# Causal self-attention on one core: the mask of the first score pass moved from TensorE to VectorE

## What is computed

```
x = _layernorm(x + _L0_attn_ref(x, L0_attn_Wq_down, ...), axis=-1)
```

## Time and profile before

| | |
|---|---|
| median of 3 runs | 2562.7 us (2561.79 to 2567.87) |
| profiled execution: time | 2562.45 us |
| profiled execution: span from the first to the last instruction | 2560.6 us |
| mean granted TensorE clock | 0.878 of full speed |
| TensorE matmuls busy | 2133.6 us (83%) |
| VectorE busy | 1537.1 us (60%) |
| ScalarE busy | 949.2 us (37%) |
| GpSimd busy | 926.3 us (36%) |
| the self-attention stage | from 0 to about 404 us of the span |

### The profile page before, as it was taken

The page is one execution under the profiler, slowest core; times in us unless marked ns, Lnnn a source line. Parts: engine busy times, 40 slices in busy tenths (PEclk is TensorE's granted clock), DMA queues, the critical chain, the costliest instruction groups (busy, mean ns, idle before and its releaser), DMA issues. The chain is left out here.

```text
span 2560.6 us, 58413 instructions
## 1 busy us (share of the span) xinstructions
PE 2133.6 (83%) x20310; PEld 1601.6 (63%) x20310; DVE 1537.1 (60%) x3500; ACT 949.2 (37%) x1881; POOL 926.3 (36%) x911
## 2 busy tenths in 40 slices
PE   5999997999776664888399996899999999997575
PEld 4666665777676563665398885566666666664233
DVE  0344443555454455333244654699999999984798
ACT  0444442333211110333124341344444444442797
POOL 0111111111144545232554531355555555553333
PEclk9999998999887776899677887899999999997555
DMA  6011003656311110876322311011000110000111
GB/s 207 26 30 30 29 25 116 217 198 215 132 50 32 37 35 24 271 241 182 92 86 78 102 39 39 26 32 32 26 28 30 32 32 30 24 20 8 53 57 46
DMA packets 157644, 192.76 MB, mean 75 GB/s; under 512 B 28517, under 2 KB 141160, under 8 KB 157559
## 3 DMA queue, kind: packets, MB, share of 16 engines
q1 hardware_dynamic: 136426, 179.73, 22.5%
q10 hardware_dynamic: 10861, 9.30, 1.2%
q0 software_dynamic: 10272, 2.62, 0.5%
HBM read 140.74 MB, written 77.51 MB: 85 GB/s over the span
## 5 line engine op out<-in xcount | busy, mean ns | idle before, releaser
L2730 ACT ACTIVATE xa_prob<-xa_A 121x1600 f32<-121x1600 f32 x96 | 144.5, 1505 | 304.2 <-PE xa_A L2609 304.2
L2801 POOL TENSOR_TENSOR xa_prob<-xa_prob,xa_exp_bias 121x1600 f32<-121x1600 f32 x64 | 228.7, 3574 | 41.0 <-ACT xa_prob L2730 40.9
L2908 DVE TENSOR_REDUCE xa_kq<-xa_A 100x4 f32<-100x1444 f32 x128 | 211.6, 1653 | 20.8 <-PE xa_A L2582 20.6
L1408 POOL DMA_INDIRECT slot_rows<-rt_x_again,rt_slot_u x150 | 151.9, 1012 | 163.8 <-DVE rt_x_again L1526 102.1
L2888 DVE TENSOR_SCALAR xa_rows_n<-xa_rows_t,xa_mv,xa_rstd 121x256 f32<-121x256 f32 x128 | 142.4, 1172 | 2.4 <-POOL xa_rstd L2818 2.4
L2609 PEld LDWEIGHTS xa_A<-xa_q2T,xa_kqT 17*121 17x121 f32 x3072 | 93.8, 185 | 56.5 <-DVE xa_kq L2908 35.9
L2582 PE MATMUL xa_A<-xa_kqT 16*100 16x361 f32 x1024 | 112.9, 510 | 10.0 <-ACT xa_prob L2730 6.8
L2609 PE MATMUL xa_A<-xa_q2T,xa_kqT 17*121 17x100 f32 x3072 | 109.3, 280 | 13.8 <-DVE xa_kq L2908 13.2
L695 DVE TENSOR_REDUCE sa_kq<-sa_A 100x16 f32<-100x1600 f32 x32 | 58.5, 1827 | 102.8 <-PE sa_A L453 102.8
L1654 POOL DMA_INDIRECT contrib<-ex_y,ex_place_u x64 | 62.4, 975 | 154.3 <-ACT ex_y L1706 135.5
L2823 POOL TENSOR_TENSOR xa_o_rstd<-xa_o_var,xa_power 100x1 f32<-100x1 f32 x32 | 17.9, 560 | 252.1 <-DVE xa_o_var L2948 252.1
(11 more groups left out here) (345 smaller groups left out, 5439.6 us busy)
## 6 DMA issues: line engine op xcount, KB each, us to landing
ex_w<-in_w13T SPq DMA_DIRECT2D x64, 352.0 KB
contrib<-xs_zero SPq DMA_DIRECT2D x30, 640.0 KB
la_rows<-contrib SPq DMA_DIRECT2D x16, 1200.0 KB
xs_ctxT<-in_ctxT SPq DMA_DIRECT2D x32, 512.0 KB
xa_rows_t<-in_ctx SPq DMA_DIRECT2D x96, 121.0 KB
ex_w<-in_w2T SPq DMA_DIRECT2D x64, 176.0 KB
slot_rows<-xs_zero SPq DMA_DIRECT2D x32, 272.0 KB
ex_x_t<-slot_rows SPq DMA_DIRECT2D x64, 136.0 KB, 2.2
```

The lines of the kernel that those rows point to most:

```text
L1408: nc.gpsimd.indirect_dma_start(slot_rows, bass.IndirectOffsetOnAxis(slot_u[:, k, n:n + 1], 0), x_again[:, k, :], None, bounds_check=SLOTS ...
L2730: nc.scalar.activation(prob[:, n, :].rearrange("p (h a) -> p h a", h=HPG), A[:ROWS, :, 0:G * T], ACT.Exp, scale=EXP_SCALE).then_inc(exp_re ...
L2801: nc.gpsimd.tensor_tensor(chunk, chunk, exp_bias[:, n, :].unsqueeze(1).to_broadcast([ROWS, HEADS, T]), ALU.mult).then_inc(biased, 1)
L2908: nc.vector.tensor_reduce(kq[:T, k, NCH, 4 * j:4 * j + 4, DH:DH + 1].rearrange("p h o -> p (h o)"), A[:T, :, 0:src_len], axis=AXIS_X, op=A ...
```

## The change

The four constant products L448 of the first pass go; its 16 score products overwrite the banks (`start=True`). VectorE adds a mask of 100 x 100 in float32 (`later_keys`, 0 or -1e30) to the 1600 columns while it copies them out of the banks to a new tile `masked` in SBUF (`mask`), and `maxima` reduces `masked` in place of the banks. A new semaphore `masked_ready` says that the banks have been read; `score_turned` waits for it in place of `max_ready`. `maxima` now stands behind `rope` in VectorE's body. One more constant is loaded at the start (19 DMAs in place of 18). The second pass keeps its four constant products.

```
--- before.py
+++ after.py
@@ -290,6 +290,8 @@
+        later_keys = s.sb("later_keys", [T, T])
+        masked = s.sb("masked", [T, HPG, G * T])
@@ -334,7 +336,7 @@
-        W_ALL = 16 * 18
+        W_ALL = 16 * 19
@@ -372,6 +374,7 @@
                 sp.dma_start(causalf[:], w["causal"]).then_inc(w_in, 16)
+                sp.dma_start(later_keys[:], w["later_keys"]).then_inc(w_in, 16)
                 rows((0, 0))
@@ -444,14 +447,11 @@
                     pe.wait_ge(kqT_ready, at(b, 2, 2))
                     pe.wait_ge(exp_ready, at(later(b, -2), 1, 1))
-                    for h in range(HPG):
-                        nc.tensor.matmul(A[:T, h, 0:G * T].rearrange("p (j t) -> p j t", t=T), causal[:],
-                                         identb[:].unsqueeze(1).to_broadcast([T, G, T]), start=True, stop=False, skip_group_check=True)
                     for j in range(G):
                         for h in range(HPG):
                             part = slice(32 * h, 32 * h + DH)
                             last = nc.tensor.matmul(A[:T, h, j * T:(j + 1) * T], kqT[part, k, j, T:2 * T], kqT[part, k, j, 0:T],
-                                                    start=False, stop=True, skip_group_check=True)
+                                                    start=True, stop=True)
                     last.then_inc(scored, 1)
@@ -470,7 +470,7 @@
                     if scores_between:
-                        pe.wait_ge(max_ready, at(later(b, 1), 1, 1))
+                        pe.wait_ge(masked_ready, at(later(b, 1), 1, 1))
@@ -688,12 +688,18 @@
+                def mask(b):
+                    dve.wait_ge(scored, at(b, 1, 1))
+                    dve.wait_ge(max_ready, at(later(b, -1), 1, 1))
+                    nc.vector.tensor_tensor(masked[:].rearrange("p h (j t) -> p h j t", t=T), A[:T, :, 0:G * T].rearrange("p h (j t) -> p h j t", t=T),
+                                            later_keys[:].unsqueeze(1).unsqueeze(1).to_broadcast([T, HPG, G, T]), ALU.add).then_inc(masked_ready, 1)
+
                 def maxima(b):
                     k = b[1] % 2
-                    dve.wait_ge(scored, at(b, 1, 1))
+                    dve.wait_ge(masked_ready, at(b, 1, 1))
                     dve.wait_ge(q2_turned, at(later(b, -2), 1, 1))
                     nc.vector.tensor_reduce(kq[:, k, 1, :, DH:DH + 1].rearrange("p (j h) o -> p j (h o)", j=G),
-                                            A[:T, :, 0:G * T].rearrange("p h (j t) -> p j h t", t=T),
+                                            masked[:].rearrange("p h (j t) -> p j h t", t=T),
                                             axis=AXIS_X, op=ALU.max).then_inc(max_ready, 1)
@@ -730,9 +736,11 @@
                     if has(-3):
                         finish(later(b, -3))
                     if has(1):
-                        maxima(later(b, 1))
+                        mask(later(b, 1))
                     if has(2):
                         rope(later(b, 2))
+                    if has(1):
+                        maxima(later(b, 1))
                     if has(-1):
                         divide(later(b, -1))
@@ -3484,6 +3492,7 @@
+    c["later_keys"] = np.where(t[None, :] <= t[:, None], 0, NEG).astype(np.float32)
```

More of the change, by code:

```diff
@@ L327, in self_attention @@
         kq_turned, kqT_ready = s.sem("kq_turned"), s.sem("kqT_ready")
-        scored, max_ready = s.sem("scored"), s.sem("max_ready")
+        scored, masked_ready, max_ready = s.sem("scored"), s.sem("masked_ready"), s.sem("max_ready")
         q2_turned, q2_ready = s.sem("q2_turned"), s.sem("q2_ready")
@@ L675, in _ @@
                 nc.vector.memset(kq[:, :, 0, :, DH:DH + 1], -1.0).then_inc(cleared, 1)
-                for sem, per in ((roped, 1), (max_ready, 1), (rec_ready, 1), (y_ready, 1), (r_ready, 1), (o_stats_ready, 1), (o_mv_ready, 1),
+                for sem, per in ((roped, 1), (masked_ready, 1), (max_ready, 1), (rec_ready, 1), (y_ready, 1), (r_ready, 1), (o_stats_ready, 1), (o_mv_ready, 1),
                                  (o_var_ready, 1), (out_ready, 1)):
```

## The result

| | before | changed |
|---|---|---|
| median of five runs | 2562.7 us (2556.24 to 2669.53) | 2539.56 us (2531.96 to 2543.56) |
| profiled execution, span | 2560.6 us | 2537.5 us |
| mean granted TensorE clock | 0.878 | 0.874 |
| ratio of the runs | | 0.9906 (95% interval 0.9884 to 0.9928) |

The run of 2669.53 us was in a slower state of the chip, which the ratio leaves out; the other four of the kernel before end at 2567.87. The change saves 0.9%, 23.1 us between the two medians as between the two spans. The forecast was 25.5 us, 2537 us. Run again beside the kernel before on another occasion, the changed kernel came to 0.9903 (0.987 to 0.9937).

The account below looks back on a forecast made before the run. The prediction took TensorE's instructions, one behind another, as the bound: -25.9 us for the products and +0.4 for the start make -25.5, from 2562.45 to 2537 us, with a range of 2533 to 2547.

Parts of the forecast that it names:

- The bound and the two places: Stage loop: TensorE, 95% busy, sets the pace; it waits before L465, and L477's two inputs come due within 0.1 us.
- The products that go: First pass on TensorE: the four constant products take 0.81 us per batch, 25.9 us less over 32 batches.
- The mask at 1.83 us: VectorE's new addition of 1600 columns takes 1.83 us, between 1.80 and 2.15, so L477 waits as before.
- The maxima at 1.80 to 1.83 us: VectorE's maxima, read from SBUF behind rope, fill 1.80 us of idle time; L702 is delayed by less than 0.1 us.
- The 0.8 us of cover: VectorE's queue behind the maxima: L713 ends 0.8 us before the second half of L439 needs its bank.
- The start, +0.4 us: Stage start: one more constant's DMA delays TensorE's first work by 0.4 us.
- The wait that stays: TensorE's 0.48 us wait for ScalarE before L465 moves with the period, neither won nor lost.
- The first batch: The four products take 1.50 us there; 0.81 was counted, the 0.7 of difference kept for the range.
- The mask was not slow: Rival, 4%: VectorE's addition takes about 3.4 us, L477 waits 1.6 us more per period; 26 us worse, 2589 us.
- The clock did not fall: Rival, 2%: TensorE's clock drops in the loop, some 8 us more per affected period; eight periods would make 2601 us.
- No gain came back as a wait: Rival, 4%: the 0.81 us returns as a wait before L465 or L439's second half; 2563 us.
- the rival with more gain: Rival, 5%: the slow-clock stretch at the stage's end goes and the first batch gives its 0.7; 2533 us or under.

Follow-up runs that it names:

- longer_release: The changed kernel with one more unused addition of 400 columns on VectorE ahead of the mask; period 10.19 us, ratio 0.9963 to the kernel before.
- products_back: The changed kernel with the first pass's four constant products put back on TensorE, VectorE's mask kept; period 10.52 us, ratio 1.0006 to the kernel before.
- changed_again: The changed kernel itself, unaltered, run again beside the kernel before; period 9.71 us, ratio 0.9903.

## Why the prediction was right, step by step

- **The bound and the two places.** TensorE's instructions one behind another; L477 due from two engines at once. Right, and longer_release shows how exact the second is: 0.48 us of 0.49 came through.
- **The products that go, -0.81 us in 32 periods.** Right: 0.81 by products_back, in which nothing else differs from the changed kernel. The period fell by 0.86; the other 0.045 us goes with VectorE's start, 0.09 us sooner in every second period, which the prediction does not have. That the form of the waits causes it is argued from the order of the instructions, not tested.
- **The mask at 1.83 us.** It took 1.825. The reduction of the same 1600 columns was the right row to go by, between 1.80 and 2.15. The estimate of 1.79 us from the Trainium skill (VectorE: DVE Perf Modes, the section on the TRN2 errata) is 0.03 us below the row.
- **The maxima at 1.80 to 1.83 us, in a gap of 1.80.** They took 1.811, and the reciprocal starts 0.04 us after its input, as before. Right. The 0.8 us of cover behind it was too small: 1.81 us of extra work made a wait of 0.68, not 1.0, and cost 0.32, since most of it was made up for by the 0.48 us that the next wait no longer took.
- **The start, +0.4 us.** Wrong, nothing of it shows. TensorE's first work starts at 17.05 us in place of 17.10:

```profile
17.05 20.69 PE L402 MATMUL sa_A<-sa_up,sa_down 128*128 128x32 f32 x96 [17.05 <-DMA sa_later_keys<-in_later_keys]
```

- **The wait that stays, 0.48 us before L465.** 12.0 us over 25 periods again. Right.
- **The first batch.** I counted 0.81 us for its products in place of the 1.50 that they took the earlier trace rows, since work that moves forward runs at the low clock. The trace shows this in full. Before:

```profile
64.82 1.11 PE L422 MATMUL sa_C<-sa_wv,sa_xT 128*100 128x256 f32 x4 [1.26 <-ACT sa_kq L580]
...
67.29 0.53 PE L465 MATMUL sa_C<-sa_ident,sa_kq 100*128 100x100 f32 x4 [0.50 <-ACT sa_kqT L611]
```

After:

```profile
56.75 1.67 PE L453 MATMUL sa_A<-sa_kqT 16*100 16x100 f32 x32 [0.65 <-ACT sa_kqT L611]
...
63.35 2.03 PE L425 MATMUL sa_C<-sa_wv,sa_xT 128*100 128x256 f32 x4 [1.26 <-ACT sa_kq L580]
...
67.07 0.54 PE L465 MATMUL sa_C<-sa_ident,sa_kq 100*128 100x100 f32 x4
```

L453 starts 1.75 us sooner than in the earlier trace rows, 1.50 of it by the products and 0.25 because the stage had come there sooner. But L425 now runs at the low level (2.03 us for 1.11; the granted clock from 64 to 66 us is 0.50, and 1.00 in the kernel before), and at L465 only 0.22 us of the lead is left. In this stretch the products' removal gained nothing that shows, less than the 0.81 that I took.

- **The rivals.** The mask was not slow. The clock did not fall: 1.00 in the loop, where the busy share stayed at 95% (221.49 of 233.00 us; I had worked out 94.1%). The Trainium skill's rule that the clock is throttled unless the engine has been busy of late (TensorE: Matmul & The Clock Gate, Part 1) therefore had no effect in the loop. No gain came back as a wait. Nor did the slow stretch at the stage's end go, as the rival with more gain had it: after the same idle time of 1.72 us before L477 the granted clock was 0.51 from 362 to 364 us, and in changed_again it stayed at 0.50 until 366, which is where that profile's stage lost most of its 1.9 us.
- **The sum.** The stage gained 26.2 us: 25.4 in the thirty periods between the first passes of the second and of the last batch, the rest at the start. About 1 us of it is VectorE's earlier start (0.045 us in each period of the loop). The 3.1 us between 26.2 and the whole lie in later stages that the change does not touch. The mechanism was right, and so was its main term. That 25.5 came within 2.4 us of 23.1 is partly luck: the cost of 0.4 at the start did not come, nor did the gain of 0.81 in the first batch, about 1 us of gain was missing, and the later stages move by more than all of these.

## What to carry to other kernels

An operation of 1.8 us on a half-idle engine was free and 0.8 us of products on the bound engine was the whole gain; but the 1.8 us of the maxima, left one place further forward in the same queue, made the kernel slower than before. So for work that moves to a half-idle engine, look for the gap at its place in that engine's queue and for who waits behind it, not for the engine's busy share. And where the bound engine has two waits one behind the other, price them together: 0.68 us lost in the first gave back up to 0.48 in the second.

## What the runs showed that was not expected

A small delay goes with the form of a wait: with a register instruction between the wait on a semaphore and the operation, VectorE started 1.12 us after L453's start in place of 1.03, and with the wait on an instruction of its own ahead of L477, TensorE started 0.15 us after VectorE's end in place of 0.06. No kernel was made to separate this from all else.

The kernel before took 2562.7 and 2559.3 us in two sets of runs, and 2427.1 and 2422.8 in two others. The chip's number on record is 2 for the set at 2559.3 and also for the one at 2427.1, and 13 for the one at 2422.8. The difference is not in the self-attention stage: the second pass starts 3.00 us after the first one's score products in products_back (the set at 2427) as in the changed kernel, and products_back's period is the changed kernel's and the products' 0.81 us. It is in the routing and experts' stages. The routing stage's first product, by its first and last start, in products_back (the set at 2427):

```profile
L1331 PE MATMUL rt_GL<-rt_gate,rt_xT x100: 275/275/474, 705.7 to 887.2; 128*128 128x64 f32 x100
```

and in changed_again (the set at 2559):

```profile
L1328 PE MATMUL rt_GL<-rt_gate,rt_xT x100: 275/275/476, 679.1 to 955.9; 128*128 128x64 f32 x100
```

181.5 us against 276.8; the first product of the experts' stage, by its first and last start, takes 154.4 against 187.1. Together that is 128 of the 132 us. What makes these stages so much slower on one occasion was not tried. It is why all comparisons here are ratios within one set, or periods of the stage itself.
